# Batch 0 normalised by VectorE ahead of the weights' preparation, cosines in single steps, and batch 0's loads in another order

## The chip, the cores and the metric

One core of a Trainium2 chip runs the whole kernel. The metric is the device time of one execution in microseconds. A core has five engines that run beside each other and wait for each other by semaphores: TensorE (PE), VectorE (DVE), ScalarE (ACT), GpSimd (POOL) and SyncE (SP), which here issues all DMAs. A group "PEld" is TensorE's loading of weights.

## What is computed

x has 8 batches of 1024 rows of 256 features, in float32. Two attention layers work on the same normalised input and their results are added to x:

```python
xn = _layernorm(x, axis=-1)
x = x + _L0_attn_ref(xn, ...) + _L0_ffn_ref(xn, ...)

# attention A: 8 heads, keys and values from a latent of 32
c_q = h_t @ W_DQ + b_DQ
c_kv = h_t @ W_DKV + b_DKV          # q, k, v are made from these; k_r = h_t @ W_KR + b_KR
attn = softmax((q . k) * scale);  o = attn @ v_c;  return o @ W_O + b_O

# attention B: 16 heads of 16, with a mask on the keys
q_n = q_pure / norm(q_pure);  qg_n = q_g / norm(q_g)
sim = (qg_n[None, None] * q_n).sum(-1).mean(-1)          # cosines with a given vector
sim = (sim - sim.min()) / (sim.max() - sim.min())        # over all batches
pos = sim > 0.9
# tokens attend to the keys of their own kind; the first 5 keys are seen by all;
# the first 5 rows are the mean of both masked attentions
```

The masks need the least and the greatest cosine over all 8 batches, so phase B of no batch can start before every batch has been projected.

## The kernel before

The kernel runs in three parts.

**Start.** SP issues the loads of x of batch 0, of 16 weights and vectors (semaphore `w_in`), and of x of batch 1. GpSimd fills constants (`filled`). When all weights are there, TensorE multiplies them with each other into products that the kernel uses (`Gk`, `Gb`, `NA`, `cst`: L1036 to L1050), and VectorE prepares `wq_x` and others beside it (L1316 to L1348). Then VectorE measures batch 0 (`measure(0)`, `invert_root(0)`), GpSimd normalises it (`normalise(0)`), TensorE transposes it (jobs `t`).

**The pass.** `pass_batch(b)` writes the jobs of one batch in an order by hand, and `pass_jobs()` joins the batches to the list `PASS`. Each engine walks through this list and does its own share of each job. A job takes one of four PSUM banks in turn (`index`), so TensorE can be up to four jobs ahead of the engine that frees the bank. Jobs are: `lat` (latent projections), `qk0` to `qk3`, `kt0`, `kt1`, `kb` (queries and keys; ScalarE rounds them and VectorE subtracts, the halves are then stored to DRAM by SP from a ring of four buffers), `v`, `va` (values), `q` (squares and dot products for the cosines), `ln`, `root`, `inv` (measuring, rooting and normalising the next batch, the last by GpSimd), `cosroot` and `cos` (the cosines of two batches, in batches 2, 4, 6 and, for the last two, 7), `draw` (the masks), `mt` (the masks' transposes), `x` (the load of a later batch), `first` (the loads of batch 0 for A, in batch 1). In batches 2 to 7 maxima of A's scores for batch 0 (`ma`, four groups of 32, VectorE reduces 128x512 each) are laid between the jobs, and each group ends with `fa`: the negated maxima are transposed, and SP takes them over DRAM into rows of QA (`shift`).

**Phases.** For each batch phase A (4 groups of 8 steps) and phase B (8 groups of 8 steps): in each step TensorE computes scores (`scores`), ScalarE exponentials, TensorE values (`values`), and for A GpSimd and TensorE add up the denominators. Between them lie the maxima of later groups (`place`): in batch 0's phase A those of B's first two groups, at steps 16 to 31. The denominators of a group go SP, DRAM, SP (`dens`), VectorE's reciprocal (`invert`, which in phase A of batch 0 stands at steps 13, 21 and 29), SP, DRAM, SP (`recs`). VectorE takes all this in one fixed order. So does SP: in `a_steps` of batch 0, group 0, it issues `load_va`, the masks, the four loads of B (`load_b`), and VB, and only then the denominators of the groups.

## Time and profile before

| | us |
|---|---|
| median of 3 runs | 3185.72 (3184.40 to 3187.57) |
| the profiled execution | 3185.31 |
| its span, first to last instruction | 3183.5 |
| TensorE busy | 2951.3 (93%) |
| VectorE busy | 2248.9 (71%) |
| ScalarE busy | 1742.0 (55%) |
| GpSimd busy | 904.7 (28%) |

The span cut in 40 slices of 80 us, busy tenths of each engine, and the granted clock of TensorE in tenths:

```profile
PE   6999986999998999899999999999989998999997
DVE  3466632788668876797679767886688767976791
POOL 4313124300550045003520163005500450025201
PEclk9999988999999999999999999999999999999999
DMA  4745445024302340225011520243023402150001
```

Batch 0's first scores of phase A fall into slice 6 (from 448.5 us), so the pass takes the slices before it. In the rows below a wait is shown behind an instruction as the idle time of its engine before it and what ended it.

### The profile page before, as it was taken

Reading aid. Unit: us, or ns where it says so; the run is one execution under the profiler, and the core shown is the slowest. Engines: PE = TensorE matmul, PEld = TensorE weight load, DVE = VectorE, ACT = ScalarE, POOL = GpSimd, SP = SyncE. Lnnn points to the kernel's source line nnn. Section 1 sums busy time; section 2 is a strip of 40 time slices with the busy share of each in tenths; the row PEclk is TensorE's granted clock in tenths of the full one; section 3 lists DMA queues with packets and bytes.
Section 4 is the critical chain, followed back from the end, with each engine's and each line's share of the span. In section 5 each row is a group of like instructions: output and inputs, shape, how many; then the busy total and the mean of one; then the engine's idle time right before and its main releaser. Section 6 shows DMA issues by size and latency. Waiting matters only on the chain.

```text
span 3183.5 us, 45721 instructions
## 1 busy us (share of the span) xinstructions
PE 2951.3 (93%) x17346; PEld 1304.0 (41%) x17346; DVE 2248.9 (71%) x4004; ACT 1742.0 (55%) x2047; POOL 904.7 (28%) x367
## 2 busy tenths in 40 slices
PE   6999986999998999899999999999989998999997
PEld 3555542333443344334433443334434443344333
DVE  3466632788668876797679767886688767976791
ACT  2333334566456655665457545665566555655574
POOL 4313124300550045003520163005500450025201
PEclk9999988999999999999999999999999999999999
DMA  4745445024302340225011520243023402150001
GB/s 142 253 181 190 165 135 93 22 57 68 73 23 60 54 87 19 64 37 107 16 46 35 95 47 20 60 68 72 23 60 54 87 19 63 37 105 19 19 14 35
DMA packets 128411, 225.01 MB, mean 71 GB/s; under 512 B 48546, under 2 KB 79170, under 8 KB 126000
## 3 DMA queue, kind: packets, MB, share of 16 engines
q1 hardware_dynamic: 128192, 222.10, 29.1%
q8 instruction: 137, 2.24, 0.3%
q14 instruction: 82, 0.67, 0.1%
HBM read 143.44 MB, written 78.32 MB: 70 GB/s over the span
## 4 chain that ended last, share of the span: by engine, by line
PE 70%; DVE 22%; DMA 2%; issue 2%; ACT 2%; SPq 1%; POOL 0%; POOLq 0%; ACTq 0%; DVEq 0%
PE O L1215 21%; DVE mx L1462 18%; PE M L1134 14%; PE M L1128 8%; PE S L1194 5%; PE S L1197 4%; PE M L1231 3%; PE M L1086 3%; PE M L1174 2%; PE M L1176 2%; PE M L1104 1%; PE M L1100 1%; PE M L1147 1%; ACT PT L964 1%; DMA den_d<-RB 1%
## 5 line engine op out<-in xcount | busy, mean ns | idle before, releaser
L1462 DVE TENSOR_REDUCE mx<-M 128x1 f32<-128x512 f32 x3036 | 1943.1, 685 | 533.3 <-PE M L1134 334.2
L964 ACT ACTIVATE PTx<-S 128x1024 f32<-128x1024 f32 x768 | 748.0, 1022 | 524.8 <-PE S L1197 308.3
L964 ACT ACTIVATE PT<-S 128x1024 f32<-128x1024 f32 x768 | 749.7, 1022 | 479.8 <-PE S L1194 241.4
L1134 PE MATMUL M<-KB,QB 50*128 50x512 f32 x2048 | 727.4, 488 | 116.1 <-DVE mx L1462 90.4
L1134 PEld LDWEIGHTS M<-KB,QB 50*128 50x128 f32 x2048 | 295.1, 185 | 829.5 <-DVE mx L1462 604.5
L1197 PE MATMUL S<-QB,KB 52*128 52x512 f32 x2048 | 460.8, 417 | 2.5 <-ACT PT L964 1.6
L1128 PE MATMUL M<-KA,QA 98*128 98x512 f32 x988 | 412.4, 458 | 15.6 <-DVE mx L1462 8.6
L836 POOL TENSOR_TENSOR SUM<-PT 128x2048 f32<-128x2048 f32 x64 | 292.8, 4575 | 421.2 <-PE M L1231 212.2
L836 POOL TENSOR_TENSOR SUM<-PTx 128x2048 f32<-128x2048 f32 x64 | 292.7, 4573 | 174.4 <-PE M L1231 174.4
L1194 PE MATMUL S<-QA,KA 114*128 114x512 f32 x1024 | 317.3, 413 | 2.4 <-ACT PT L964 2.4
L1128 PEld LDWEIGHTS M<-KA,QA 98*128 98x128 f32 x988 | 168.3, 188 | 308.0 <-issue 182.4
L1215 PE MATMUL O<-PT,VB 128*32 128x512 f32 x2048 | 280.2, 619 | 0.0
L1197 PEld LDWEIGHTS S<-QB,KB 52*128 52x128 f32 x2048 | 250.8, 188 | 68.0 <-issue 43.5
L1215 PE MATMUL O<-PTx,VB 128*32 128x512 f32 x2048 | 274.9, 608 | 0.7 <-ACT PTx L964 0.7
L1194 PEld LDWEIGHTS S<-QA,KA 114*128 114x128 f32 x1024 | 182.5, 190 | 82.6 <-issue 41.4
L860 POOL TENSOR_TENSOR OB<-OB,RB 128x512 f32<-128x512 f32 x32 | 41.1, 1284 | 576.7 <-DMA RB<-recb_d 550.9
L854 POOL TENSOR_TENSOR OS<-OS,RB 128x512 f32<-128x512 f32 x32 | 41.1, 1283 | 573.0 <-DMA RB<-recb_d 573.0
L1215 PE MATMUL O<-PT,VA 128*32 128x512 f32 x1024 | 138.2, 612 | 3.7 <-issue 3.7
L1215 PE MATMUL O<-PTx,VA 128*32 128x512 f32 x1024 | 136.4, 605 | 0.0
L1231 PE MATMUL M<-SUM,ones 128*32 128x512 f32 x1024 | 133.8, 594 | 2.4 <-POOL SUM L836 2.4
L1486 DVE RECIPROCAL RC<-RC 128x16 f32<-128x16 f32 x96 | 23.3, 243 | 100.7 <-DMA RC<-den_d 100.7
L802 POOL TENSOR_SCALAR PTx<-PT,early 128x256 f32<-128x256 f32 x64 | 77.3, 1223 | 59.0 <-DVE early L1309 59.0
(189 smaller groups left out, 1915.8 us busy)
## 6 DMA issues: line engine op xcount, KB each, us to landing
KA<-kt_d SPq DMA_DIRECT2D x48, 512.0 KB, 7.1
QB<-qk_d SPq DMA_DIRECT2D x192, 128.0 KB
KB<-qk_d SPq DMA_DIRECT2D x192, 128.0 KB
qk_d<-QB SPq DMA_DIRECT2D x16, 1024.0 KB, 4.1
kt_d<-QB SPq DMA_DIRECT2D x16, 1024.0 KB, 4.6
RB<-recb_d SPq DMA_DIRECT2D x64, 256.0 KB
vb_d<-VB SPq DMA_DIRECT2D x8, 1536.0 KB, 5.1
VB<-vb_d SPq DMA_DIRECT2D x8, 1536.0 KB, 12.9
```

Source lines behind the costliest of these rows:

```text
L802: last = nc.gpsimd.tensor_scalar(xn[:, i, c, :], xin[:, i, c, :], mv[i][:, c, 0:1], rstd[i][:, c:c + 1], ALU.subtract, ALU.mult)
L836: nc.gpsimd.tensor_tensor(SUM[:, :, :], probs(k - 1), probs(k), ALU.add).then_inc(summed, 1)
L964: nc.scalar.activation(probs(k)[:, 2 * pair:2 * pair + 2, :], Sg[pair][:, :].rearrange("p (j s) -> p j s", j=2), ACT.Exp, scale=SCALE_A if ...
L1086: done = mm(m[0:rows, :], w[:, k, :], xnT[b % 2][:, k, hf * HALF:(hf + 1) * HALF], start=(k == 0), stop=(k == KD - 1))
L1128: done = mm(m[:, :], QA[0:A_MAX_ROWS, at:at + P], KA[0:A_MAX_ROWS, 4 * q + 2 * a + e, keys], start=True, stop=True)
L1134: done = mm(m[:, :], QB[rows, 2 * q + a, at:at + P], KB[rows, 2 * q + a, keys], start=True, stop=True)
L1174: mm(m[:, 0:D], OA[:, q, at:at + P], NA[:, q, :], start=(q == 0), stop=False)
L1194: last = mm(to, KA[0:A_ROWS, 4 * q + 2 * pair + e, ks], QA[0:A_ROWS, qs], start=True, stop=True)
L1197: last = mm(to, KB[rows, 2 * q + pair, ks], QB[rows, 2 * q + pair, qs], start=True, stop=True)
L1215: last = mm(O[32 * jj:32 * jj + 32, :], lhs, probs(step)[:, jj, :], start=(c == 0), stop=(c == NC - 1), skip_group_check=True)
L1231: last = mm(DN[32 * jj:32 * jj + 32, :], ones32[:, :], SUM[:, jj, :], start=(c == 0), stop=(c == 3), skip_group_check=True)
L1462: v.tensor_reduce(mx[:, g % 2, unit, kh:kh + 1], m[:, :], AX.X, ALU.max).then_inc(free, 1)
```

## The change

- `normalise(0)` by GpSimd is gone. VectorE measures batch 0, takes the inverse root and normalises (8 TENSOR_SCALAR of 128x256) ahead of everything that it does with the weights; TensorE's and ScalarE's jobs `t` of batch 0 (the first two of `PASS`) come ahead of the weights' products. The root of the weights' norms now comes second on ScalarE.
- The block `cos` becomes eight jobs `("cos", lo, part)`: two reciprocals of half the columns, five elementwise operations, and one reduction. One is put behind every job from `kt0` on (batches 2, 4 and 6) or from `qk0` on (batch 7); later the maxima are laid between them. GpSimd's all-reduce comes with the last part, so behind the `cq` split; `draw` comes behind the first four `v`.
- The shift of A's last group (`fa`, 3) comes ahead of `mt` and `qk3` of batch 7 and not at the very end. TensorE's first scores wait for all four shifts of batch 0.
- SP: the load of VA goes to job `first`; of B's four loads only the first stays ahead of the masked part of group 0, the second comes behind the denominators of group 0, the last two behind those of group 1.

```diff
@@ pass_batch
-    s += [("root", b + 1)] if more else [("cosroot", 6), ("cos", 6)]
+    s += [("root", b + 1)] if more else [("cosroot", 6)]
-    s += [("cos", b - 2)] if b in (2, 4, 6) else []
     s += [("va", b), ("qk1", b, 0), ("qk1", b, 1)]
+    s += [("v", b, c) for c in range(4)]
     s += [] if more else [("draw",)]
-    s += [("v", b, c) for c in range(4)] + [("kt1", b, 0), ("kt1", b, 1)] + (q[4:6] if more else [])
+    s += [("kt1", b, 0), ("kt1", b, 1)] + (q[4:6] if more else [])
...
+    lo = {2: 0, 4: 2, 6: 4, 7: 6}.get(b)
+    if lo is not None:
+        at = s.index(("kt0", b, 0) if more else ("qk0", b, 0))
+        for part in range(COS_PARTS):
+            s.insert(at + 1 + 2 * part, ("cos", lo, part))
@@ pass_jobs
+            if b + 1 == B:
+                jobs.insert(len(jobs) - 4, ("fa", "a", GA - 1))
             for i in reversed(range(len(mine))):
-                at = 3 + i * (len(jobs) - 4) // len(mine)
+                at = 3 + i * (len(jobs) - (4 if b + 1 < B else 10)) // len(mine)
-    return out + [("fa", "a", GA - 1)]
+    return out
@@ sync, first
                 load_a(0, 1)
+                wait_apart(sp, va_out[0], 16)
+                load_va(0)
@@ sync, a_steps, not before and g == 0
-                    load_va(0)
                     masks_out()
                     load_b(0, 0)
-                    load_b(0, 1)
-                    for i in range(RING):
-                        wait_apart(sp, st_out[i], NUSE * B * 16)
-                    load_b(0, 2)
-                    load_b(0, 3)
                     wait_apart(sp, vb_out, B * 16)
                     load_vb(0)
...
                 elif before:
                     recs(b, "b", GB - 1)
+                if not before and g == 1:
+                    load_b(0, 1)
+                if not before and g == 2:
+                    for i in range(RING):
+                        wait_apart(sp, st_out[i], NUSE * B * 16)
+                    load_b(0, 2)
+                    load_b(0, 3)
@@ gpsimd
-        normalise(0)
@@ scalar
-        act.wait_ge(root_in, 1)
-        nc.scalar.activation(small[:, 32:48], small[:, 16:32], ACT.Sqrt).then_inc(root_out, 1)
         passing(("root", 0))
-        for j in PASS:
+        for j in PASS[:2]:
+            passing(j)
+        act.wait_ge(root_in, 2)
+        nc.scalar.activation(small[:, 32:48], small[:, 16:32], ACT.Sqrt).then_inc(root_out, 1)
+        for j in PASS[2:]:
             passing(j)
@@ tensor, scores
-                    pe.wait_ge(sha_in, n * (GA * 16) + (g + 1) * 16)
+                    pe.wait_ge(sha_in, max(GA, n * GA + (g + 1)) * 16)
@@ tensor (the weights' products stand between the two loops now)
+        pe.wait_ge(const_ready, 1)
+        for j in PASS[:2]:
+            passing(j)
+        pe.wait_ge(w_in, N_W)
+        pe.wait_ge(xt_ready, 1)
...
-        for j in PASS:
+        for j in PASS[2:]:
             passing(j)
@@ vector, ahead of dve.wait_ge(w_in, N_W)
+        measure(0)
+        invert_root(0)
+        dve.wait_ge(inv_done, 1)
+        for f in range(2):
+            for c in range(4 * f, 4 * f + 4):
+                last = v.tensor_scalar(xn[:, 0, c, :], xin[:, 0, c, :], mv[0][:, c, 0:1], rstd[0][:, c:c + 1],
+                                       ALU.subtract, ALU.mult)
+            last.then_inc(xn_done, 1)
@@ vector, cosines(lo, part)
+            y, x, t = root[:, cols], n2[:, cols], newton[:, cols]
+            if part == 0:
+                own.link(v.reciprocal(y[:, 0:half], y[:, 0:half]))
+            elif part == 1:
+                own.link(v.reciprocal(y[:, half:2 * half], y[:, half:2 * half]))
+            elif part == 2:
+                own.link(v.tensor_tensor(t, y, y, ALU.mult))
...
```

## Rows read from the trace of the kernel before

**Rows 1.** The page: busy time of each engine, share of the span, instructions.

```profile
PE 2951.3 (93%) x17346; PEld 1304.0 (41%) x17346; DVE 2248.9 (71%) x4004; ACT 1742.0 (55%) x2047; POOL 904.7 (28%) x367
```

**Rows 2.** Timeline, the start: start, us, engine, line, operation [idle before].

```profile
11.13 2.66 POOL L791 MEMSET VB<- 128x3072 f32 x1
...
17.59 0.54 PE L1040 MATMUL S<-early 128*97 128x33 f32 x2 [17.59 <-DMA halves<-in_halves]
...
32.65 0.43 DVE L1348 TENSOR_TENSOR cst<-M,early 128x256 f32<-128x256 f32 x1 [4.89 <-PE M L1049]
...
38.08 9.70 POOL L802 TENSOR_SCALAR PTx<-PT,early 128x256 f32<-128x256 f32 x8 [23.28 <-DVE early L1309]
...
43.10 1.94 PE L1063 MATMUL S<-ident,PTx 128*128 128x128 f32 x8 [10.49 <-POOL PTx L802]
...
49.60 4.53 PE L1086 MATMUL M<-SUM,Wlat 128*96 128x512 f32 x8
```

**Rows 3.** One line's instructions: the two loads of batch 0's x, issued from 0.74.

```profile
DMA to landing us min/median/max: 4.0/4.5/5.0
```

**Rows 4.** Windows, TensorE alone: stretch, length, busy (count), granted clock, DMA share, GB/s.

```profile
49.60:51.60 2.00, 2.00 (x4) 0.53 0.93 325
```

**Rows 5.** Timeline, batch 4: first, second and last cosine operation, then TensorE.

```profile
257.41 1.73 DVE L1303 RECIPROCAL early<-early 128x256 f32<-128x256 f32 x1
...
259.17 0.78 DVE L1304 TENSOR_TENSOR early<-early 128x256 f32<-128x256 f32 x1
...
261.70 0.42 DVE L1375 TENSOR_REDUCE early<-early 128x16 f32<-128x256 f32 x1
...
262.90 2.35 PE L1104 MATMUL M<-Wqkv,SUM 128*128 128x256 f32 x5 [2.28 <-DVE OB L1443]
```

**Rows 6.** Timeline of SP: last stores of batches 1, 2 and 3.

```profile
139.94 0.36 SPq L528 DMA_DIRECT2D qk_d<-stg  x1
...
191.91 0.36 SPq L528 DMA_DIRECT2D qk_d<-stg  x1
...
238.93 0.36 SPq L528 DMA_DIRECT2D qk_d<-stg  x1
```

**Rows 7.** Timeline of batch 7, and the window behind its block of cosines.

```profile
406.67 0.43 DVE L1304 TENSOR_TENSOR early<-early 128x256 f32<-128x256 f32 x1
...
409.98 0.38 POOL L827 PARTITION_ALL_REDUCE early<-early  x1 [46.47 <-DVE early L1385]
...
410.49 2.08 PE L1093 MATMUL O<-latT,Gk 97*128 97x512 f32 x2 [3.96 <-DVE mx L1462]
...
418.59 2.35 POOL L817 TENSOR_TENSOR OB<-latT,OB 32x1024 fp32r<-32x1024 f32 x1 [7.32 <-issue]
...
411.00:421.00 10.00, 10.00 (x21) 0.50 0.26 105
```

**Rows 8.** Timeline, start of phase A; last the chain of waits.

```profile
448.54 1.17 PE L1194 MATMUL S<-QA,KA 114*128 114x512 f32 x4
...
457.03 1.94 PE L1215 MATMUL O<-PT,VA 128*32 128x512 f32 x8 [3.68 <-issue]
...
465.30 4.57 POOL L836 TENSOR_TENSOR SUM<-PTx 128x2048 f32<-128x2048 f32 x1 [6.21 <-PE M L1231]
...
450.68 3.68 DMA sh_d<-sh
```

**Rows 9.** Timeline of SP, TensorE and VectorE, the chain of waits, and a window.

```profile
468.56 1.24 SPq L559 DMA_DIRECT2D QB<-qk_d  x3
...
500.38 26.34 DMA den_d<-RB
...
529.53 1.38 PE L1134 MATMUL M<-KB,QB 50*128 50x512 f32 x2 [25.90 <-DVE mx L1462]
...
583.83 0.24 DVE L1486 RECIPROCAL RC<-RC 128x16 f32<-128x16 f32 x1
...
480.00:488.00 8.00, 7.28 (x42) 1.00 1.04 136
```

More of the change, by code:

```diff
@@ L1238, in of_batch @@
             return b if own else n
-        for j in PASS:
+        pe.wait_ge(const_ready, 1)
[3 more added lines that the diff above has]
+        pe.wait_ge(xt_ready, 1)
+        for h in range(HA):
+            g = Sg[0][0:97, 64 * h:64 * h + 33]
+            mm(g, Lp[:, h, :], Rp[:, h, :], start=True, stop=False)
+            last = mm(g, sel[0:CA, :], KRp[0:CA, h, :], start=False, stop=True)
+        last.then_inc(setup_pe, 1)
+        for h in range(HA):
+            j, q = h % 4, h // 4
+            last = mm(M[1 + q][32 * j:32 * j + 32, 0:D], Wuv[:, h, :], Wo[:, h, :], start=True, stop=True)
+        last.then_inc(setup_pe, 1)
+        pe.wait_ge(setup_dve, 1)
+        for h in range(HA):
+            last = mm(M[0][:, 0:D], buvb[:, h, :], Wo[:, h, :], start=(h == 0), stop=(h == HA - 1))
+        last.then_inc(setup_pe, 1)
+        pe.wait_ge(setup_dve, 2)
+        for j in PASS[2:]:
             passing(j)
@@ L1314, in inverse, with measure, invert_root @@
                 last.then_inc(ready, 1)
+        def measure(b):
+            dve.wait_ge(x_in[b % 2], b // 2 * 32 + 32)
+            if b >= 2:
+                dve.wait_ge(xn_done, 2 * (b - 2) + 2)
+            for c in range(NC):
+                own.link(v.bn_stats(stats[:, c, :], xin[:, b % 2, c, :]))
+            own.settle()
+            for c in range(NC):
+                own.link(v.bn_aggr(mv[b % 2][:, c, :], stats[:, c, :]))
+            own.settle()
+            v.tensor_scalar(var, mv[b % 2][:, :, 1], EPS, None, ALU.add).then_inc(root_in, 1)
+        def invert_root(b):
+            dve.wait_ge(root_out, b + 2 if b else 1)
+            inverse(rstd[b % 2], var, tiny, inv_done)
+        measure(0)
[6 more added lines that the diff above has]
+            last.then_inc(xn_done, 1)
         dve.wait_ge(w_in, N_W)
@@ L1418, in passing @@
             elif kind == "cos":
[L1419 to L1420 removed]
+                cosines(j[1], j[2])
+                if j[1:] == (B - 2, COS_PARTS - 1):
                     extremes()
```

69 lines of the change are left out of this document (23 added, 46 removed).

## Prediction

> **What bounds the kernel now.** I read the page first, then the timeline and the chain of waits where TensorE stands still, since it is busy for 93% of the span [rows 1] and an engine beside it matters only where it makes it wait. Over the steady loops the diff changes nothing but a constant in one wait, which the later batches exceed anyway. What it touches is the first 530 us: the start, the pass over the batches (all projections), and the first phase A. There the reader is to see four kinds of lost TensorE time. (1) At the start TensorE works on the weights from 17.59 us, VectorE's last step of that ends at 33.08, and then a chain follows: statistics, root, GpSimd's normalisation (9.70 us), transposes; batch 0's first projection starts only at 49.60 [rows 2]. (2) In three batches of the pass VectorE does the cosines in one block, and TensorE stands for 2.3 us behind it [rows 5]. (3) In the last batch the same block and GpSimd's all-reduce stop TensorE for 4.0 us, and the granted clock is 0.50 (1.2 of 2.4 GHz) behind it [rows 7]. (4) In the first phase A a DMA of 8 KB of denominators needs 26.3 us to land, and TensorE stands for 25.9 us [rows 9].
>
> **The start.** x of batch 0 is issued first and lands 4.0 to 5.0 us after its issue [rows 3], so by about 6.2 us. Then come VectorE's statistics and inverse root, which take from the end of the weights' part at 33.08 to the start of GpSimd at 38.08, 5.0 us [rows 2]: to 11.3. The normalisation moves from GpSimd to VectorE. Before has no such instruction on VectorE; the nearest row is its TENSOR_TENSOR of 128x256, 0.43 us [rows 7], so 8 take 3.4 us at most: 14.7. Eight transposes take 1.94 us at the low clock [rows 2]; the second eight end by 16.9, and ScalarE's copy of them can run beside the weights' work. The weights are there only at 17.59, when TensorE starts now [rows 2]. So all that is moved ahead is covered by that wait, with 0.7 us to spare. The weights' part then goes as now to 33.1, and the first projection follows it: 49.60 - 33.1 = 16.5 us gained. The first projection also ran at a granted clock of 0.53 over its first 2 us [rows 4], as TensorE had stood idle since 32.6; right behind the weights' work it should not: 1 us more. Together **-17.5**. Bounds: a GpSimd memset of VB lies on 11.13 to 13.79 [rows 2], and the normalisation could be held behind it for up to 2.7 us. Less the 0.7 of slack, that costs 2.0. The other way, transposes right ahead of the weights could bring the high clock earlier for the weights' 15.5 us. It is already high by their end, and what VectorE prepares in between limits the gain, to 5 us as an estimate (a third of the 15.5); I take neither.
>
> A row that speaks against work on VectorE beside GpSimd: VectorE's TENSOR_TENSOR on two SBUF inputs took 0.78 us in batch 4, where GpSimd was normalising, and 0.43 in the last batch, where it was not [rows 5, 7]. The Trainium skill has the rule (SBUF — State Buffer, section "Who interferes with whom"): the two engines share one pair of SBUF ports as an exclusive lock, taken by a VectorE tensor_scalar in its two-port mode, and by one with two SBUF inputs against a GpSimd operation that reads SBUF; the later one waits for the whole of the other. The trace agrees in this one instruction. By that rule the memset holds the normalisation, the start gives -15.5, and cosines laid beside GpSimd's normalisation wait again and again; by the rows alone they wait 0.35 us once.
>
> **Batch 0's loads of A.** At batch 1 SP issues the loads of KA and QA and now the one of VA as well (128 KB), ahead of batch 1's store of kt. At the 136 GB/s of the slowest stretch [rows 9] this is 1 us, at the best nothing: I take **+0.5**: ScalarE waits for that store and TensorE for ScalarE. At the start of phase A it goes away.
>
> **Cosines in batches 2, 4 and 6.** From SP's last store of a batch to the next one, batch 2 takes 191.91 - 139.94 = 51.97 us and batch 3, which has no cosines, 47.02 [rows 6]: one block costs 4.95 us, more than the 2.3 us of idle time [rows 5]. The same 4.7 us of work (257.41 to 262.12) [rows 5] now lies in eight pieces between the jobs of the pass; none is over 0.9 us (half of the 1.73 us reciprocal). With four PSUM banks between TensorE and VectorE such a piece is covered. But VectorE's own work stays: over the 15 or so jobs that the pieces are laid between it is about as long as TensorE's. And the pieces start earlier, when GpSimd still normalises the next batch (9.70 us) [rows 2], so up to four of them can wait for an instruction of 1.2 us. I take 3 of the 5 us back, in three batches: **-9**; bounds 0 and -15.
>
> **The last batch.** The idle 4.0 us, and 10 us (411 to 421) at the granted clock of 0.50 behind it, in which up to 5 us of work was lost [rows 7]: 9 us at most. GpSimd's split of cq comes ahead of the all-reduce instead of behind it. But the all-reduce takes from 409.98 to 418.59, 8.6 us [rows 7], and VectorE's masks wait for it; between the last cosine piece and the masks now lie ten jobs, some 8 to 10 us of TensorE's work. Besides, VectorE has more to do than TensorE up to that point. I give 2.5 us back: **-6.5**; bounds -2 and -10.
>
> **The start of phase A.** Now scores start at 448.54 at once, but the first values wait for VA until 457.03, and GpSimd's second sum, which sets the pace of the first 16 steps, starts at 465.30 [rows 8]. After the change VA is there. In its place TensorE waits, ahead of the first score, for all four shifts. The last one is taken just after the last v job, some 4 us before the end of the pass; VectorE takes 0.6, the way to DRAM 3.7 [rows 8], the way back, which the rows don't show, at most as much; I take 2.5. So the scores start some 3 us after the pass. From there to the second sum it takes about 10 us: four exponentials, the first sum of 4.6 [rows 8] and its denominators. That is 13 us after the pass, against 465.30 - 448.54 = 16.8: **-3**, bounds 0 and -5. Behind TensorE's wait nothing else of its queue could run.
>
> **The stall.** SP issues all four loads of B (each 12 DMAs of 128 KB and 4 of 16 KB, 1.6 MB) from 468.56 on, and den_d, the first group's denominators, behind them at 500.38; it lands at 526.7 [rows 9]. VectorE waits for it ahead of its reciprocal, and the maxima of step 16 are queued behind that reciprocal, so TensorE stands until 529.53 [rows 9]. At 136 GB/s [rows 9] one load takes 12 us. Times from here on count from the end of the pass. The first load starts 20 us in as now [rows 9] and, with VB (1.5 MB) behind it, is through after some 20 more; den_d, 52 us in now, is issued behind these two alone and lands by 40. TensorE stopped at 503.6, 55 us in, early in step 16; 3 less by the start of the phase, so step 16 comes 50 us in, and its maxima no longer wait. Gained: 25.9, and 2 us of low clock behind the idle time as at the start. What is late next: the 13 steps from 16 to VectorE's reciprocal of step 29 took 583.83 - 529.53 = 54.3 us [rows 9], less 2 for the clock, so 4 us each. Loads 2 and 3 are issued behind the reciprocal of step 21, at 74, and need 24 us, to 98. The shift of B's first group (ready at 86) and the denominators of A's third group stand behind them in SP's order and land at 101 to 103.5. The shift is needed at step 32, at 114; VectorE asks for the denominators at step 29, at 102. So 1 us is lost: **-27**; bounds -20 and -28. Load 1 (issued behind the first group's denominators, at 45, so there at 57) is needed at step 24, at 82.
>
> **Sum.** -17.5 + 0.5 - 9 - 6.5 - 3 - 27 = -62.5 us. The span of 3183.5 becomes 3121, the profiled run's 3185.3 becomes 3122.8, and its difference to the median of 3185.7 is noise; I say **3122**.
>
> **Rivals.**
> (a) The stall moves instead of going: loads 2 and 3 run slower than 136 GB/s beside the phase's own traffic, and the denominators for step 29 land late. For: the stretch was at this rate with nothing else in flight [rows 9]. Against: I count 1.5 us against it, not 26. With loads of 18 us each VectorE waits 12 us more: 3134. The Trainium skill (DMA: Bandwidth & Descriptors, section "Queues, rings and completion order") says that each DMA engine takes one issuer's descriptors in their order, which is what this rival lives on; den_d's 26.3 us agree. Chance 0.12.
> (b) VectorE is the bound in the pass: pieces or block, 4.7 us of cosines cost the same, and the masks wait for the all-reduce. This is also how the change would not do what it says. For: 0.78 against 0.43 us above. It takes back 9 + 4.5: 3136. Chance 0.15; this is where the rule on the shared ports above would lead.
> (c) The clock is high through the weights' work and the cosines are free: -5 and -5 more, 3112. Chance 0.12.
> (d) Slower than before: the second half of B's loads, moved behind step 21, isn't there when phase B starts at step 32, and TensorE waits for the shift behind it. It decides once TensorE waits over 69 us at step 32 (62.5 to lose the gain, 6 to be told): loads issued from 74 on would have to end after 183, 3.2 MB in 109 us, 29 GB/s instead of 136 [rows 9]; then 3192. Nothing in the profile comes near. Chance 0.02.
> The forecast has the rest, 0.59.
>
> **Range and chances.** The bounds of the single costs don't fall together: I let two at a time reach theirs. Down, the cosines and the weights' clock give 6 + 5 and the last batch 3.5: 3107. Up, cosines and last batch cost 9 + 4.5 and the stall 7: 3142. That takes in (b) and most of (a) and (c). A measurement of this kernel tells 0.2% (6 us) from no change. Faster by more: 0.97; within it 0.01; slower 0.02.
>
> **What would show it.** In the trace of the changed kernel: the transposes end before the weights arrive at 17.6, and batch 0's first projection starts at 33 to 34 (not 49.6); the same spacing of SP's stores in batches 2 and 3, within 2 us; no TensorE idle time over 2 us in the last batch, and the pass ends near 416 (448.5 less 32.5); den_d lands within 3 us of its issue; no wait of TensorE over 5 us from there on, so step 32 comes some 114 us after the pass. The forecast is wrong if the weights' part starts late behind the transposes, if batches 2, 4 and 6 still take 52 us, or if VectorE's reciprocal at step 21 or 29 waits for its DMA.

## The result, and the profile after

The changed kernel took 3134.39, 3139.74 and 3154.40 us, against 3184.4 to 3191.22 for the kernel before; a fourth run, of 4995.63 us, was disturbed and is left out of the ratio. The ratio is 0.9861, with a 95% interval of 0.9818 to 0.9903. Forecast were 3122, with a range of 3107 to 3142. The median of all four runs, 3147.07, is some 40 us below that of before (3186.64 on the same chip) and 5 us above the range. The median of the first three, 3139.74, lies just inside it; six more runs of the same kernel, the first experiment below, have a median of 3146.12, outside again. So the sign is right and the size is not.

The profiled run took 3134.39 us, with a span of 3132.6. Its rows, in the order of the prediction. The page, busy time (against [rows 1]):

```profile
PE 2942.3 (94%) x17346; PEld 1299.2 (41%) x17346; DVE 2250.2 (72%) x4016; ACT 1741.2 (56%) x2047; POOL 896.3 (29%) x359
```

The timeline of the start (start, us, engine, line, operation, idle before), against [rows 2]. VectorE normalises from 11.24, TensorE transposes from 15.76 (16 matmuls, both halves), the weights' products begin at 19.20 and batch 0's first projection at 33.84 instead of 49.60:

```profile
11.13 2.66 POOL L802 MEMSET VB<- 128x3072 f32 x1
...
11.24 5.66 DVE L1353 TENSOR_SCALAR PTx<-PT,early 128x256 f32<-128x256 f32 x8
...
13.85 0.98 POOL L802 MEMSET QA<- 32x1024 f32 x1
...
15.76 3.65 PE L1057 MATMUL S<-ident,PTx 128*128 128x128 f32 x16 [15.76 <-DVE PTx L1353]
...
19.20 0.42 PE L1241 MATMUL S<-early 128*97 128x33 f32 x2
...
33.84 3.67 PE L1080 MATMUL M<-SUM,Wlat 128*96 128x512 f32 x8 [0.52 <-DVE cst L1389]
```

The timeline of SP: the last stores of batches 1, 2 and 3, against [rows 6]. The distances are 51.46 and 47.00 us, where before had 51.97 and 47.02: batch 2 with its cosines is as long as it was.

```profile
123.52 0.36 SPq L536 DMA_DIRECT2D qk_d<-stg  x1
...
174.98 0.36 SPq L536 DMA_DIRECT2D qk_d<-stg  x1
...
221.98 0.36 SPq L536 DMA_DIRECT2D qk_d<-stg  x1
```

Batch 2 in windows (stretch, length, busy time and count of TensorE, its weight loads, VectorE, ScalarE and GpSimd, granted clock, DMA share, GB/s). The pieces of the cosines lie in the first of these stretches:

```profile
131.80:149.00 17.20, 14.41 (x40) 6.45 (x41) 14.69 (x29) 5.13 (x12) 10.19 (x8) 0.90 0.43 149
149.00:175.00 26.00, 25.78 (x100) 17.02 (x99) 13.59 (x21) 11.04 (x25) 0.00 (x0) 1.00 0.45 182
```

VectorE is busy for 85% of the first stretch and 52% of the second; TensorE misses 2.8 us of the first, in five waits of under 0.8 us each, all ended by VectorE, and its clock falls there all the same.

The timeline of the last batch and of the start of phase A, against [rows 7] and [rows 8]: the all-reduce, the masks' first operation, the first score, the last two of the first four exponentials (to 433.6), GpSimd's first sum, the denominators behind it.

```profile
401.96 0.37 POOL L837 PARTITION_ALL_REDUCE early<-early  x1 [19.35 <-DVE early L1425]
...
410.28 0.14 DVE L1430 TENSOR_SCALAR early<-early 128x1 f32<-128x1 f32 x1
...
428.07 2.08 PE L1188 MATMUL S<-QA,KA 114*128 114x512 f32 x4 [3.41 <-DMA QA<-sh_d]
...
431.67 1.94 ACT L975 ACTIVATE PT<-S 128x1024 f32<-128x1024 f32 x2 [0.40 <-PE S L1188]
...
441.08 4.48 POOL L846 TENSOR_TENSOR SUM<-PT 128x2048 f32<-128x2048 f32 x1 [38.75 <-issue]
...
445.71 1.08 PE L1225 MATMUL M<-SUM,ones 128*32 128x512 f32 x4 [7.18 <-POOL SUM L846]
```

The timeline of the place where TensorE stood for 25.9 us, against [rows 9]: SP issues the first, second and third group's denominators, TensorE begins step 16, VectorE inverts the third group's.

```profile
466.91 0.56 SPq L603 DMA_DIRECT2D den_d<-RB  x1
...
485.32 0.49 PE L1128 MATMUL M<-KB,QB 50*128 50x512 f32 x2
...
491.86 0.51 SPq L603 DMA_DIRECT2D den_d<-RB  x1
...
533.24 0.52 SPq L603 DMA_DIRECT2D den_d<-RB  x1
...
538.18 0.24 DVE L1526 RECIPROCAL RC<-RC 128x16 f32<-128x16 f32 x1
```

From these rows and those of before the way from start to end divides at the same points of both programs. The end of the pass is the first score less the idle time before it: 428.07 - 3.41 = 424.7 (448.5 before, where there was none).

| stretch | before, us | after, us | difference | forecast |
|---|---|---|---|---|
| start to batch 0's last store | 91.4 | 74.8 | -16.6 | -17.5 |
| batch 1 | 48.6 | 48.8 | +0.2 | +0.5 |
| batches 2, 4, 6 | 158.5 | 158.7 | +0.2 | -9 |
| batches 3, 5 | 93.9 | 93.9 | 0 | 0 |
| last batch, to the end of the pass | 56.1 | 48.4 | -7.7 | -6.5 |
| end of the pass to step 16 | 53.6 | 60.7 | +7.1 | -3 |
| step 16 to the reciprocal of step 29 | 81.7 | 52.9 | -28.8 | -27 |
| from there to the end | 2599.7 | 2594.4 | -5.3 | 0 |
| sum | 3183.5 | 3132.6 | -50.9 | -62.5 |

Two terms are wrong by 9 and 10 us, and a third, over 2600 us in which the program is the same, was not in the forecast. The experiments go to these three, and to whether the four terms that look right are right for the reasons given.

### The profile page after: what moved, and what is told of

It reads as the page before. It is cut to its first block, busy times and chain, and to the rows that moved or that the text cites. A ratio compares the mean times of both kernels' runs of the same rounds, so it can differ in the third digit from the quotient of the medians.

```text
span 3132.6 us, 45726 instructions
## 1 busy us (share of the span) xinstructions
PE 2942.3 (94%) x17346; PEld 1299.2 (41%) x17346; DVE 2250.2 (72%) x4016; ACT 1741.2 (56%) x2047; POOL 896.3 (29%) x359
## 4 chain that ended last, share of the span: by engine, by line
PE 71%; DVE 22%; issue 2%; ACT 2%; DMA 1%; POOL 1%; SPq 0%; POOLq 0%; ACTq 0%; DVEq 0%
PE O L1209 22%; DVE mx L1502 19%; PE M L1128 14%; PE M L1122 8%; PE S L1188 5%; PE M L1225 4%; PE S L1191 4%; PE M L1080 3%; PE M L1168 2%; PE M L1170 2%; PE M L1141 1%; PE M L1098 1%; PE M L1094 1%; ACT PT L975 1%; POOL SUM L846 1%
## 5 line engine op out<-in xcount | busy, mean ns | idle before, releaser
L1188 PEld LDWEIGHTS S<-QA,KA 114*128 114x128 f32 x1024 | 182.9, 190 | 85.5 <-issue 40.2
L1521 DVE TENSOR_TENSOR XR<-M,XR 128x256 f32<-128x256 f32 x64 | 27.2, 425 | 91.6 <-PE M L1170 91.6
L1168 PE MATMUL M<-NA,OA 128*128 128x256 f32 x256 | 72.7, 407 | 17.3 <-POOL OB L867 13.2
```

Of the source, the lines that this page charges most:

```text
L1168: mm(m[:, 0:D], OA[:, q, at:at + P], NA[:, q, :], start=(q == 0), stop=False)
L1188: last = mm(to, KA[0:A_ROWS, 4 * q + 2 * pair + e, ks], QA[0:A_ROWS, qs], start=True, stop=True)
```

## The experiments

"Low clock" below is the time for which the trace grants TensorE 1.2 instead of 2.4 GHz, summed over its clock records.

### The changed kernel again

No edit. 

> The changed kernel once more, unaltered, to see how far its runs lie apart. The first runs gave 3134.4, 3139.7 and 3154.4 us. Theory A (the spread is time at the low clock): spans and mean granted clock move together, a run 20 us longer has a mean clock about 0.006 lower. Theory B (a wait of varying length, at the same clock): the clock does not follow the time. Either: profile with batch 0's first projection at 33.8, GpSimd's first sum at about 441, and batches 2, 4 and 6 taking 51.5 to 55.5 us.

Measured: 3146.12 us, median of 6 (3138.8 to 3151.25), against 3183.9 of before on the same chip (11 runs, 3176.88 to 3197.35); ratio 0.9878, interval 0.9856 to 0.9901. So the gain is 1.2% (38 us), and the first profiled run was at the fast end. Its profile (span 3145.2) has the same distances between stores (51.65 and 47.00 for batches 2 and 3), the first sum at 440.15 and step 16 at 484.43, 0.9 earlier than the first one. It is 12.6 us longer than the first one, and by step 16 it was 0.9 ahead: 13.5 us came in behind. 3.0 of them lie between step 16 and the reciprocal of step 29, with a wait for the third group's denominators, and 10.5 behind it. Of the two theories the first holds: over the nine runs of this kernel the mean granted clock falls, in the main, as the time rises, from 0.984 at 3134.39 us to 0.978 at 3154.4, which is the 0.006 expected for 20 us. Timeline of VectorE:

```profile
540.33 0.25 DVE L1526 RECIPROCAL RC<-RC 128x16 f32<-128x16 f32 x1 [2.89 <-DMA RC<-den_d]
```

### GpSimd's first operation behind the all-reduce

In the profile after, the first sum starts at 441.08, though the last of its exponentials ended at 433.6. It is GpSimd's first instruction behind the all-reduce. Before, the late one was the subtraction in the split of cq, by 7.32 us [rows 7]. A row of before shows that neither the all-reduce's own length nor just any operation behind it is meant: the first half of the split, a CAST with one input, stood right behind the all-reduce's 409.98 and started at once. Timeline of GpSimd, before:

```profile
410.24 1.03 POOL L815 CAST OB<-latT 32x1024 fp32r<-32x1024 f32 x1
```

The edit puts a small operation of the same kind (128x16) in between, where nobody waits for it:

```diff
+                pool.wait_ge(dum_in, 1)
+                nc.gpsimd.tensor_tensor(dum[:, :], dum[:, :], dum[:, :], ALU.add).then_inc(dum_in, 1)
```

> The changed kernel with one TENSOR_TENSOR of 128x16 on an unused tile put on GpSimd right behind its all-reduce. In the changed kernel the first sum of phase A starts at 441.08, though its last exponential ended at 433.6, and it is GpSimd's first operation behind the all-reduce at 401.96; before, the subtraction of the cq split was the one that came 7.3 us late. Theory A (GpSimd needs some 7.4 us before its first two-input operation behind the all-reduce): the new operation takes that wait, far ahead of phase A; the first sum starts at 433 to 434, step 16 comes 7 us earlier, and the time is 7 us lower. Theory B (the sum is late for something at the start of phase A, as its instructions being fetched or the DMAs of the masks): the sum stays at about 441 and the time does not move.

Measured: 3137.56 us, median of 4 (3126.23 to 3144.24), ratio 0.9847 (0.9813 to 0.9882). Timeline of GpSimd:

```profile
401.85 0.38 POOL L841 PARTITION_ALL_REDUCE early<-early  x1 [19.35 <-DVE early L1431]
409.39 0.20 POOL L844 TENSOR_TENSOR sb_dum<-sb_dum 128x16 f32<-128x16 f32 x1 [7.16 <-issue]
433.63 4.59 POOL L852 TENSOR_TENSOR SUM<-PT 128x2048 f32<-128x2048 f32 x1 [24.04 <-ACT PT L981]
```

The small operation now bears the delay, 7.16 us, and the sum starts 7.45 us earlier, released by ScalarE. Step 16 comes at 476.57 instead of 485.32, 8.7 us earlier. The median is 8.6 us below that of the changed kernel on the same chip (3146.12), where 7 were expected; the two intervals overlap. That the delay belongs to the first two-input operation behind the all-reduce, and not to the sum, is shown. It doesn't belong to every first one either: at the start of the changed kernel, where no all-reduce has run yet, the split's subtraction follows its CAST without a wait (39.59). What stands ahead of the gap is a pair of records of GpSimd's sequencer, on the line of the late operation. One line's instructions, the changed kernel's sum:

```profile
L846 POOLq MODIFY_POOL_CONFIG  x2: 11/11/11, 433.8 to 433.9; - x2
```

All thirteen profiles have this pair ahead of the first two-input operation behind the all-reduce, whichever it is, and that operation starts 6.7 to 7.6 us behind the pair; the CAST of before has none ahead of it. Beside it the Trainium skill has a sentence (GPSIMD Engine Reference, section "Instruction dispatch"): the first call to a freshly loaded kernel pays for a load of about 6 us that no instruction of the profile shows. The pair fits that; its length here is more than 6 us, and that code is loaded in it no row shows.

### The fourth shift taken earlier

TensorE waits 3.41 us at the first score for the last batch's fourth shift. The edit:

```diff
-                jobs.insert(len(jobs) - 4, ("fa", "a", GA - 1))
+                jobs.insert(len(jobs) - 8, ("fa", "a", GA - 1))
```

> Of the changed kernel one job is moved: VectorE takes the last batch's fourth shift ahead of the last four v jobs instead of behind them. Theory (the way of this shift through DRAM is the 3.4 us for which TensorE waits at the first score): the first score follows the end of the pass within 0.5 us instead of 3.6. The first sum of GpSimd doesn't move by as much: it is late for another reason (it starts 39.1 us after the all-reduce's row), so it comes at 440 to 441 again, and step 16 at 484 to 485.5; the time stays within 1 us. Rival (the sum follows the scores): it comes at 437.6 and step 16 at 482.

Measured: one run, 3150.29 us. The wait is gone: the first score starts at 423.14, 0.1 us behind the end of the pass. But the expectation on the sum was wrong, and its rival right. Timeline of ScalarE (the first four exponentials) and of GpSimd:

```profile
425.00 3.79 ACT L975 ACTIVATE PT<-S 128x1024 f32<-128x1024 f32 x4
...
436.00 4.48 POOL L846 TENSOR_TENSOR SUM<-PT 128x2048 f32<-128x2048 f32 x1 [34.98 <-issue]
```

The exponentials end at 428.8 and the sum starts at 436.0, again 7.2 us later, though 35 us have passed since the all-reduce (38.75 in the profile after). So the delay doesn't run down while GpSimd waits: it begins once the inputs of the first such operation are there. Taken together, the shift and the delay are 3.4 and 7.4 us, both on the path. The small operation helps because its inputs are ready long before those of the sum.

### The pieces of the cosines, elsewhere and not at all

Two edits on the same question: do single operations between other jobs cost less than a block? In the first, the pieces of batches 2, 4 and 6 come behind the v jobs, in the stretch in which VectorE is busy for only half of the time:

```diff
-        at = s.index(("kt0", b, 0) if more else ("qk0", b, 0))
+        after = [("v", b, c) for c in range(NC)]
         for part in range(COS_PARTS):
-            s.insert(at + 1 + 2 * part, ("cos", lo, part))
+            at = s.index(after[part]) if more else s.index(("qk0", b, 0)) + 2 * part
+            s.insert(at + 1, ("cos", lo, part))
```

> The changed kernel with the eight cosine pieces of batches 2, 4 and 6 put behind the eight v jobs of their batch instead of behind kt0 and what follows. The v jobs are freed by ScalarE and leave VectorE idle. Theory A (VectorE is the bound in the stretch from kt0 to qk1, so pieces there cost as much as the block; among the v jobs it has room): batches 2, 4 and 6 take 47.5 to 49 us instead of 51.5, 51.6 and 55.7, and the time is 8 to 11 us lower. Theory B (the pieces cost what they cost wherever they lie, by the ports shared with GpSimd or by the clock): 51 to 52 us stay, and the time is within 3 us.

Measured: 3133.41 us, median of 4 (3127.44 to 3140.22), ratio 0.9840 (0.9812 to 0.9868), 12.7 us below the changed kernel on the same chip, where 8 to 11 were expected. In the second, all eight operations are one block again, in these batches ahead of va and in the last one ahead of the first qk job:

```diff
-        at = s.index(("kt0", b, 0) if more else ("qk0", b, 0))
         for part in range(COS_PARTS):
-            s.insert(at + 1 + 2 * part, ("cos", lo, part))
+            s.insert(s.index(("va", b) if more else ("qk0", b, 0)), ("cos", lo, part))
```

> The changed kernel with the cosines as one block again: ahead of va in batches 2, 4 and 6, and ahead of qk0 in batch 7, so GpSimd's all-reduce comes ahead of its cq split again. Theory A (spreading is worth nothing in batches 2, 4 and 6, and in batch 7 it gives 7 us but takes 7 back at GpSimd's first sum): batches 2, 4 and 6 within 1 us of 51.5, 51.6 and 55.7; batch 7's pass 6 to 8 us longer; the first sum follows its last exponential within 0.5 us; the time is within 3 us of the changed kernel's. Theory B (the forecast's): batches 2, 4 and 6 take 3 us more each, and the time is 12 to 15 us higher.

Measured: one run, 3145.83 us. Timelines of SP, last stores of batches 1 and 2, of the pieces behind the v jobs and then of the block:

```profile
123.20 0.36 SPq L537 DMA_DIRECT2D qk_d<-stg  x1
...
171.26 0.36 SPq L537 DMA_DIRECT2D qk_d<-stg  x1
```

```profile
120.85 0.36 SPq L535 DMA_DIRECT2D qk_d<-stg  x1
...
172.09 0.36 SPq L535 DMA_DIRECT2D qk_d<-stg  x1
```

Batch 2 takes 48.06 us behind the v jobs, 51.46 as the change has it, and 51.24 as a block. In batches 4 and 6 the block is 0.9 and 2.0 us shorter than the pieces (50.74 and 53.66 against 51.63 and 55.66), so 2.0 is more than the 1 us expected at most. To spread the work brings nothing; to put it where VectorE has time brings 3.4 us in batch 2, 3.6 in batch 4 and 3.6 in batch 6. Windows of batch 2 with the pieces behind the v jobs, against those of the profile after (columns as there):

```profile
131.50:147.00 15.50, 13.75 (x47) 7.19 (x48) 11.81 (x22) 6.09 (x14) 9.66 (x8) 1.00 0.51 170
147.00:171.20 24.20, 23.96 (x93) 15.67 (x92) 16.33 (x28) 10.06 (x23) 0.00 (x0) 1.00 0.48 193
```

VectorE's busy time moved: 2.9 us less in the first stretch, 2.7 more in the second, where TensorE still misses only 0.2 us of 24.2. And the clock no longer falls (1.00 instead of 0.90). That is the larger part of the gain: over the two stretches TensorE does the same 140 matmuls in 37.7 us of busy time instead of 40.2, which is 2.5 us, and only 1.0 us less of idle time is added to it. A clock of 0.90 over 17.2 us is worth 1.7 us of these, as an estimate.

A rival was that the pieces beside GpSimd's normalisation are slow by the ports that VectorE shares with it. The rows are against it: in batch 2 the reciprocals take 0.94 us each beside it and 0.94 and 0.95 behind the v jobs, the elementwise operations with two inputs 0.40 to 0.46 and 0.42 to 0.43. It is GpSimd that takes longer, 10.19 us for its eight operations instead of 9.66.

The block shows a second thing: in the last batch, where before and this version have the block, the way from the store of batch 6 to the end of the pass is 56.7 us, against 48.4. Timeline of the block's last batch, GpSimd and then TensorE:

```profile
398.88 2.35 POOL L827 TENSOR_TENSOR OB<-latT,OB 32x1024 fp32r<-32x1024 f32 x1 [7.29 <-issue]
...
405.79 5.49 PE L1097 MATMUL M<-Wqkv,OA 128*128 128x256 f32 x12 [4.69 <-DVE OB L1482]
```

The delay of 7.3 us is back at the split of cq, whose subtraction now is the first two-input operation behind the all-reduce, and TensorE waits for 4.7 us; in exchange the first sum is late no more: it starts at 435.80, and the last of its exponentials ends at 435.62. The change moved this one delay from the last batch to phase A; it didn't remove it.

### The order of B's loads alone

```diff
                     load_b(0, 0)
+                    load_b(0, 1)
+                    for i in range(RING):
+                        wait_apart(sp, st_out[i], NUSE * B * 16)
+                    load_b(0, 2)
+                    load_b(0, 3)
                     wait_apart(sp, vb_out, B * 16)
```

and the same three taken out behind the first and the second group. 

> Of the changed kernel only the order of B's loads is undone: all four are issued behind the fourth step of phase A, ahead of the first group's denominators. Theory (the queue of SP was the stall): the first denominators land some 25 us after their issue instead of 2, and the way from TensorE's step 16 to VectorE's reciprocal of step 29 takes 81 us as in the kernel before (81.7) instead of 54.5; the time rises by 25 to 27 us, to about 3172. Rival (the later start of the first sum has moved the denominators so far back that the loads are through by then): they land after 15 us or less and the 13 steps take under 70 us.

Measured: one run, 3157.84 us. Chain of waits, then the timeline of TensorE:

```profile
474.62 26.17 DMA den_d<-RB
```

```profile
503.39 1.38 PE L1126 MATMUL M<-KB,QB 50*128 50x512 f32 x2 [16.68 <-DVE mx L1500]
```

The queue is the cause: with the old order den_d takes 26.2 us again (26.34 before [rows 9]). But TensorE stands for 16.7 us, not 25.9, and the way from step 16 to the reciprocal of step 29 takes 71.8 us, between the 81.7 and the 52.9. den_d is issued 50.2 us behind the end of the pass (51.9 before), but step 16 comes 60.8 us behind it and not 53.6: with the first sum late, the stall begins later and ends no later (79.0 us behind the end of the pass, 81.0 before). The expectation of 25 to 27 us more was wrong, and so was its rival, which had the denominators land sooner. By these numbers the late sum would have been free, had the loads stayed, and the order of the loads alone is worth 71.8 - 52.9 = 18.9 us in this program. The ledger's -28.8 and +7.1 are two ends of one matter.

### The normalisation: which engine, and beside what

First, GpSimd clears VB behind VectorE's normalisation instead of beside it:

```diff
         for i, (where, value) in enumerate(fills):
+            if i == 5:
+                pool.wait_ge(xn_done, 2)
```

> Of the changed kernel only GpSimd's order is changed: it clears VB behind VectorE's normalisation of batch 0 instead of beside it. Theory (VectorE is held by the memset): the eight operations take 3.4 us or less instead of 5.66, the transposes are through before 17.6 us, the weights' products start at 17.6 instead of 19.2, and batch 0's first projection at 32.2 to 33 us instead of 33.8. Rival (the operations cost 0.7 us each on VectorE by themselves): 5.7 us again, and a start at 33.8. Of the time itself (1 to 1.6 us) nothing can be seen.

Measured: one run, 3156.2 us (its clock is below). Timeline of VectorE, GpSimd and TensorE:

```profile
11.34 2.67 DVE L1355 TENSOR_SCALAR PTx<-PT,early 128x256 f32<-128x256 f32 x8
...
14.14 2.66 POOL L804 MEMSET VB<- 128x3072 f32 x1 [3.06 <-DVE PTx L1355]
...
31.92 3.67 PE L1082 MATMUL M<-SUM,Wlat 128*96 128x512 f32 x8 [0.52 <-DVE cst L1391]
```

Eight operations take 2.67 us without a memset beside them and 5.66 with. One line's instructions in the changed kernel's profile (shortest, median and longest in ns) show where the 3.0 us between them lie:

```profile
L1353 DVE TENSOR_SCALAR PTx<-PT,early x8: 395/400/2691, 11.2 to 16.5; 128x256 f32<-128x256 f32 x8
```

The first operation starts beside the memset of VB and takes 2.69 us; it ends at 13.94, 0.15 us behind that memset. The second starts beside the next memset, of QA (13.85, 0.98 us), and ends at 14.97, again 0.15 us behind it; the other six take 0.40 each. So VectorE lost 2.3 us to the one and 0.7 to the other. The trace of the change thus agrees with the rule on the shared ports that the prediction named (the Trainium skill, SBUF — State Buffer, section "Who interferes with whom"), for a memset, which reads nothing, against a one-input operation. It was worth 1.9 us: the first projection starts at 31.92 instead of 33.84.

Second, the engine is undone, the early order kept: GpSimd normalises batch 0 behind its memsets.

```diff
-        for f in range(2):
-            for c in range(4 * f, 4 * f + 4):
-                last = v.tensor_scalar(xn[:, 0, c, :], xin[:, 0, c, :], ...)
-            last.then_inc(xn_done, 1)
+        normalise(0)                       # in GpSimd's queue, ahead of its loop
```

> Of the changed kernel only the engine of batch 0's normalisation is undone: GpSimd does it, behind its memsets, and everything else at the start stays early. Theory: the memsets end at 14.8 us, the eight operations take 9.7 us as in the kernel before (to 24.5), the transposes (3.7 us) stand in TensorE's order ahead of the weights' products, so these start at 27 to 28.2 instead of 19.2 and batch 0's first projection at 41.5 to 42.7 instead of 33.8: of the 16.6 us gained, the change of engine is worth 8 to 9, the order the rest. Rival (VectorE's statistics of the weights now run ahead and shorten the weights' part): 38 to 40 us.

Measured: one run, 3158.05 us. Timeline of GpSimd and TensorE:

```profile
14.90 10.13 POOL L813 TENSOR_SCALAR PTx<-PT,early 128x256 f32<-128x256 f32 x8
...
26.85 0.43 PE L1242 MATMUL S<-early 128*97 128x33 f32 x2
...
41.00 3.67 PE L1081 MATMUL M<-SUM,Wlat 128*96 128x512 f32 x8 [0.52 <-DVE cst L1385]
```

Both numbers are below what was expected (26.85 against 27 to 28.2, 41.00 against 41.5 to 42.7). Of the 15.8 us by which the first projection starts earlier, 7.2 (41.00 - 33.84) come from the engine and 8.6 (49.60 - 41.00) from the order. For the engine 8 to 9 were expected.

### Where the rest of the spread comes from

The profiled runs differ by up to 22 us in a part of the program that is the same in all of them, from the reciprocal of step 29 to the end. Against the low clock in that part (without the last such stretch, of 13.7 to 17.1 us, which every run has at its very end):

| kernel | reciprocal of step 29 to the end, us | low clock in it, us |
|---|---|---|
| changed, first profile | 2594.4 | 44.4 |
| before | 2599.7 | 54.6 |
| B's loads undone | 2599.0 | 54.6 |
| small operation | 2601.8 | 66.6 |
| pieces behind the v jobs | 2603.2 | 69.0 |
| changed, again | 2604.9 | 71.7 |
| GpSimd normalises | 2607.2 | 75.1 |
| block | 2609.5 | 81.9 |
| shift earlier | 2610.9 | 88.7 |
| memset moved | 2613.8 | 95.6 |
| load 2 with load 1 (below) | 2603.3 | 61.4 |
| four edits (below) | 2599.8 | 58.0 |
| five edits (below) | 2594.9 | 44.4 |

A straight line through the thirteen has 0.37 us of time for each us of low clock, and all lie within 2 us of it. The line is a correlation; no run sets the clock alone. What decides how much low clock a run gets isn't shown: no edit reaches this part, and two runs of the same kernel have 44.4 and 71.7. Of the ledger's last line, -5.3, this rate explains 3.8 (10.2 us of low clock less); the same program runs there before and after.

The other thing that the profiles share is the wait for the third group's denominators at step 29. In the first profile of the changed kernel they were issued at 533.24, in time. Nine profiles have the change's order of loads: this one, the one of the version with four edits below, and those of the changed kernel again, the small operation, the shift, the two kinds of cosines, the memset and GpSimd's normalisation. In the last seven VectorE waits for them, 1.9 to 5.8 us, and TensorE behind it, 1.2 to 5.1 us. So it was with the memset moved (VectorE's timeline; then one window, columns as above, of this kernel and, last, of the changed kernel's first profile):

```profile
540.57 0.25 DVE L1528 RECIPROCAL RC<-RC 128x16 f32<-128x16 f32 x1 [4.45 <-DMA RC<-den_d]
```

```profile
510.00:533.00 23.00, 22.81 (x125) 9.53 (x121) 16.11 (x28) 12.75 (x15) 14.97 (x4) 1.00 0.93 143
```

```profile
510.00:533.00 23.00, 22.82 (x122) 9.51 (x122) 16.15 (x28) 12.83 (x14) 14.92 (x5) 1.00 0.74 156
```

Loads 2 and 3 lie in these 23 us; all traffic together moves at 143 GB/s in the one and 156 in the other. Why one run's loads are faster isn't shown. I tried to take the wait away by moving load 2 up to load 1:

```diff
                 if not before and g == 1:
                     load_b(0, 1)
-                if not before and g == 2:
                     for i in range(RING):
                         wait_apart(sp, st_out[i], NUSE * B * 16)
                     load_b(0, 2)
+                if not before and g == 2:
                     load_b(0, 3)
```

> In all profiled runs of the changed load order but two (the first profile of the changed kernel and the version with four edits), SP issues the denominators of A's third group only at 530.7 to 537.1 us, behind loads 2 and 3 of B and the shift, and TensorE stands for 1.2 to 5.1 us behind them with a low clock after it. One edit: load 2 goes with load 1, behind the first group's denominators, and only load 3 stays behind the second group's. Theory (24 us of transfers in one piece are too long for the 30 us between two groups): loads 1 and 2 end by 502, the second group's reciprocal at 507 doesn't wait, the third group's denominators are issued by 525, TensorE's wait at 535 to 541 is gone, and step 16 to the reciprocal of step 29 takes 52.9 to 53.5 us, not 55.9 to 58.8. Rival (the wait only moves to the second group): the reciprocal at 507 comes later than 508.5, and the 53 us are not reached.

Measured: one run, 3144.04 us. SP issues the third group's denominators at 529.05 (by 525 was expected), the reciprocal comes at 538.88 without a wait, and the way from step 16 to it takes 52.9 us, as the theory had it; the second group's reciprocal, at 508.35, doesn't wait either. The span is 3142.2 with 61.4 us of low clock behind step 29. But two of the nine profiles without this edit have no wait either, so one run can't show that the edit took it away, and it doesn't show that the kernel is faster.

### The edits together

> Four edits of the changed kernel together: a small two-input operation of GpSimd behind the all-reduce, the cosine pieces of batches 2, 4 and 6 behind the v jobs, the last shift taken earlier, and VB cleared behind the normalisation. By the single runs: the start -1.2, batches 2, 4 and 6 -10.5, the first score -3.3, the first sum -7.5, together 22 us less at step 16 (463 instead of 485), and 3124 instead of 3146. If the sum then waits for VectorE's or ScalarE's work instead, step 16 comes at 467 to 470 and the time is 3130.

Measured: 3118.29 us, median of 5 (3114.14 to 3124.86), ratio 0.9805 (0.9786 to 0.9823). Timeline of GpSimd and TensorE in its profile (span 3114.1):

```profile
418.48 4.58 POOL L855 TENSOR_TENSOR SUM<-PT 128x2048 f32<-128x2048 f32 x1 [21.10 <-ACT PT L984]
...
461.42 0.50 PE L1137 MATMUL M<-KB,QB 50*128 50x512 f32 x2
```

Step 16 comes at 461.4, where 463 was expected, and the time is 6 us below the 3124 expected. The single gains up to step 16 add up. The fifth edit on top, load 2 with load 1:

> The version with four edits and, as a fifth, load 2 of B together with load 1. That version reached 3118.29 us (0.9805 of the kernel before). In its profile the third group's denominators were in time by 1 us; where they aren't, 3 to 6 us are lost. Theory: the same start, 463 or less at step 16, 53 us from there to the reciprocal of step 29, and 3114 to 3118 us. If the median stays within 3 us of 3118, the waits were no part of that version's median.

Measured: 3119.67 us, median of 6 (3112.9 to 3126.22), ratio 0.9802 (0.9778 to 0.9826): the same as with four, and not the 3114 to 3118 expected. Timeline of VectorE:

```profile
486.71 0.25 DVE L1535 RECIPROCAL RC<-RC 128x16 f32<-128x16 f32 x1 [2.83 <-DMA RC<-den_d]
```

Here the wait only moves: the second group's denominators are late by 2.8 us instead, and the reciprocal of step 29 comes at 519.21, where the version with four edits has 514.28 (57.8 us behind step 16, where 53 were expected). The version with four edits is the one to keep.

## Why the prediction was right or wrong

**The start, -17.5: right (-16.6), by a sum whose errors in part cancel.** The chain was as told: covered by the wait for the weights but for the last part. VectorE's instruction costs 0.33 us and not the 0.43 taken from its neighbour, and two memsets held it for 3.0 us, where the bound had one and 2.7. The weights' part began 1.6 us late, but took 14.6 us where it took 15.5, at a clock of 1.00 in both, so not by the clock of rival (c); and the first projection ran at a clock of 1.00, as forecast. The engine was worth 7.2 us and the order 8.6.

**Cosines in batches 2, 4 and 6, -9: wrong, +0.2.** The step that failed is "with four PSUM banks between TensorE and VectorE such a piece is covered". Its own next sentence said why it would fail: over those jobs VectorE's work is as long as TensorE's. The windows show 14.69 of 17.20 us for VectorE there, and TensorE with 2.8 us of waits, all for VectorE, and a clock of 0.90. A place with room lies 10 to 16 us further on in the same batch, and there 3.5 us of the 5 came back, more by the clock than by the waits. This was rival (b), in its first half: pieces or block cost the same. I gave it 0.15, against a row of mine that spoke for it. Its other ground, waits beside GpSimd by the shared ports, didn't bear out: the pieces were as short there as elsewhere.

**The last batch, -6.5: near in size (-7.7) by luck, wrong in its reason.** I read 409.98 to 418.59 as the all-reduce's duration, 8.6 us, and let the masks wait for it, at 2.5 us. The row shows 0.38 us, and the next operation in GpSimd's queue, the CAST, had started at 410.24; the masks' first operation, at 410.28, stands right behind VectorE's maxima and waits for nothing. What took the time was the operation behind that, the split's subtraction, and its row had said so: 7.32 us of idle time, ended by "issue" and by no engine. Masks that wait were the second half of rival (b), and that half fell.

**The start of phase A, -3: wrong, +7.1.** The same misreading. If the all-reduce takes 8.6 us, nothing is left over for phase A; if the delay goes with the first two-input operation behind it, moving the split ahead of the all-reduce hands the delay to the next one in GpSimd's queue, and this was the first sum, which sets the pace. I had named "GpSimd's first sum" and "the all-reduce" in two steps and never asked what stands behind the all-reduce once the split is gone. With the small operation in between, the stretch takes 476.57 - 424.55 = 52.0 us, against 53.6 before: -1.6, which is half of the forecast. The first score started 3.4 us after the pass, where 3 was forecast.

**The stall, -27: right (-28.8) for the profiled run.** den_d landed within 2 us of its issue. Of the 28.8, 25.9 are the stall; 2.9 are left, where the forecast had 2 for the low clock behind it. "What is late next" was right in its place, the third group's denominators at step 29, but too small: 1 us, where TensorE lost 1.2 to 5.1 us in seven profiles of nine. It is rival (a) at a tenth of its size to a half, with all traffic together at 143 to 156 GB/s, of which the loads are a part, where I had given the loads 136 of their own. The loads' order on its own is worth 18.9 us: the sum being late and the stall overlap.

**Behind step 29, 0: not in the range.** The forecast let the steady loops be the same, and they are, but for the clock. Between runs of one kernel this alone is worth 10 us, and I had made the range from the bounds of the terms only. The medians of after, 3146.12 and 3147.07, lie 12 to 13 us above its first profiled run. The second profiled run shows two reasons, 10.5 us behind step 29 and 3.0 for the wait at it; before's profiled run was near its own median.

Summed up: the profiled run's span missed the forecast of 3121 by 11.6 us: cosines +9.2, start of phase A +10.1, start of the kernel +0.9, batch 1 -0.3, last batch -1.2, stall -1.8, the part behind step 29 -5.3. The median missed by 25. So the two terms that failed are the cosines (work called covered that was not) and the start of phase A (a delay of GpSimd that was taken for the all-reduce's length). Of the three signs that I had named, two came in the first profiled run: the weights' part started 1.6 us late behind the transposes, and batches 2 and 4 took 51.5 and 51.6 us, batch 6 55.7. The third, a reciprocal that waits for its DMA, came in seven profiles of nine.

## What to carry to other kernels

When an operation moves away from behind an expensive one, ask who stands there next: a wait "until issue" of several microseconds can belong to the place in the engine's queue and not to the operation that shows it. The records of that operation's line are worth a look, and here the wait could be given to a dummy where nobody waits. Work is hidden only in a stretch where its own engine has time left; cutting it into pieces didn't make that time here, so read the windows of that engine first and choose the place by them. And two stalls in a row on one path overlap: the price of each is known only with the other one there or gone.

## What the hardware showed that I had not expected

- The first two-input operation of GpSimd behind the PARTITION_ALL_REDUCE started 6.8 to 7.8 us after its inputs were ready, over thirteen profiles: however small it was (128x16: 6.81 to 7.31 us) and however long after the all-reduce (35 to 41 us for the sums). A pair of MODIFY_POOL_CONFIG records stands ahead of it. The all-reduce itself shows 0.38 us, a CAST behind it started at once, and so did the next sums.
- Two memsets of GpSimd each held one TENSOR_SCALAR of VectorE until their end: 5.66 us for eight beside them, 2.67 alone. So 0.33 us an operation, where GpSimd took 1.2 (9.70 for eight).
- One program had 44.4 and 71.7 us of low TensorE clock in the same 2600 us of two runs, and was 10.5 us longer in the second; over thirteen profiles it is 0.37 us for each.
